# A decoder of six stages on one core: earlier first product, three changed orders, and cross-attention with its PSUM banks dealt out anew

## The chip, the core and the metric

The kernel runs on one core of a Trainium2 chip, in one launch. The time is that of the device, in microseconds: the median of 3 runs, 1364.35 us (1364.26 to 1366.4). The core has TensorE (PE, matrix products and transposes, results in PSUM only), VectorE (DVE), ScalarE (ACT), GpSimd (POOL) and SyncE (SP, which issues transfers here). Each runs its own list of instructions in order, and they wait for each other on semaphores. PSUM has eight banks, each with 512 float32 a partition; the kernel keeps two engines out of one bank at a time by waits.

## The reference

x holds 16 blocks of 128 tokens with 256 channels, ctx the same of context. Six residual layers follow each other:

```
x = x + channel_attention(layernorm(x))          # softmax over channels, 256x256 scores per block
x = x + cross_attention(layernorm(x), ctx)       # 32 heads of 8, RMS-normalised q and k
x = x + quantised_linear(layernorm(x))           # rounded activations and weight
x = x + linear_attention(layernorm(x))           # 16 heads, decay, gate, group norm
x = x + gated_convolution(ctx, ctx, layernorm(x))
x = x + grouped_attention_and_experts(layernorm(x))  # 16 heads on 4 key heads; 8 experts, 2 per token
```

Cross-attention, with the block's 128 tokens and 128 context rows:

```
q = x @ Wq.T ; kv = ctx @ [Wk; Wv].T  (k and v interleaved)
q, k = rmsnorm(q), rmsnorm(k)         # over the 8 channels of a head
out = softmax(q k^T / sqrt(8)) v
```

## The kernel before

Each stage is a function with one list a stage for each engine, and ends with a barrier of all engines. The stages are: the first loads, channel attention (names `ca.`), cross-attention with the quantised linear layer (`xa.`, `ql.`), linear attention (`la.`), the convolution (`cv.`), grouped attention with the router (`ga.`), and the experts (`ex.`). TensorE's first work in them is at 15.53, 145.79, 334.64, 512.88, 611.71 and 1113.34 us.

A stage is a software pipeline over the 16 blocks. `steps` calls `step(s)` for each s, from some lead steps on to some steps behind the last, and in it `s.back(1)` is the block one earlier, `s.back(-1)` the one after. So a step works on several blocks, and the order of the parts within `step` is the order on the engine. `upto(b)` is the semaphore's value once block b is done. There is no planner: what stands first in the code is first on its engine, and whatever stands behind a wait waits too.

**Loads** (lines 215 to 236). SyncE issues x in three parts (blocks 0, 1 to 3, 4 to 15). ScalarE issues the identity and four weights. All four weights count into one semaphore, and TensorE waits for 64 of it before its first instruction (line 392). The next stages' weights follow on SyncE at once (from line 287).

**Channel attention.** In a step TensorE does the transpose of xn (line 400), psc for the block before (408), pout for the one before that (418), then pqk and pv (426, 432), and pmix (442), which waits for wo. wo is made by VectorE (342) from the row sums of ScalarE's exponentials (374), and these need the negated maxima (324, 326) of psc. VectorE does the addition of pout to x (320) ahead of the maxima.

**Cross-attention.** The bank `turn` serves in a step for the transposed xn, for pv's product with the probabilities (po) and for the v product; `turn2` for the transposed q and k, later for the turned output; `pqk` for q and k side by side. q and k are copied to raw and squared (668, 671), VectorE sums the squares (604), GpSimd takes ten operations for the root (106 to 124), and VectorE scales to `qkn` (586). TensorE turns it (724), VectorE spreads qT (597), and ScalarE copies kT (663). These two read one bank, so ScalarE waits for VectorE.

**Grouped attention.** For a block there are five products k/q (`kq`, 1717), each rotated: VectorE by cos (1551), ScalarE swaps the halves (`swap`, 1635 and 1636), GpSimd adds up (1498, 1506). The four rounds r of the block before go scores, exponentials, transposes, values (paT, 1742), `copy_aT` (1658). The output product (1761) needs all four aT.

## Time and profile before

| | us |
|---|---|
| median of 3 runs (lowest, highest) | 1364.35 (1364.26, 1366.4) |
| profiled execution | 1367.16 |
| its span, first to last instruction | 1364.7 |
| TensorE busy (matrix products) | 1186.6 (87%) |
| TensorE busy (weight loads) | 832.2 (61%) |
| VectorE busy | 765.1 (56%) |
| ScalarE busy | 577.8 (42%) |
| GpSimd busy | 603.6 (44%) |

The mean granted clock of TensorE is 0.955 of 2.4 GHz. Each stage has other limits, so the shares over the whole say little. In 700 to 1080 us, within grouped attention, TensorE is busy for 361.37 of 380 us; in 180 to 400 us, most of it cross-attention and linear attention, for 182.15 of 220. A wait costs time only where the engine that waits is the one that sets the pace. Times of matrix products in the timeline include the last one's way through the array, so the next may begin before the end shown.

### The profile page before, as it was taken

Reading aid. Unit: us, or ns where it says so; the run is one execution under the profiler, and the core shown is the slowest. Engines: PE = TensorE matmul, PEld = TensorE weight load, DVE = VectorE, ACT = ScalarE, POOL = GpSimd, SP = SyncE. Lnnn points to the kernel's source line nnn. Section 1 sums busy time; section 2 is a strip of 40 time slices with the busy share of each in tenths; the row PEclk is TensorE's granted clock in tenths of the full one; section 3 lists DMA queues with packets and bytes.
Section 4 is the critical chain, followed back from the end, with each engine's and each line's share of the span. In section 5 each row is a group of like instructions: output and inputs, shape, how many; then the busy total and the mean of one; then the engine's idle time right before and its main releaser. Section 6 shows DMA issues by size and latency. Waiting matters only on the chain. (4 is left out here: it accounts for less than half of the span.)

```text
span 1364.7 us, 24627 instructions
## 1 busy us (share of the span) xinstructions
PE 1186.6 (87%) x7421; PEld 832.2 (61%) x7422; DVE 765.1 (56%) x1930; ACT 577.8 (42%) x1504; POOL 603.6 (44%) x752
## 2 busy tenths in 40 slices
PE   4888588885899969978999999999999859999995
PEld 3666355563555534436878888878888626665663
DVE  2444368875788857984566666666666532222221
ACT  1333266663333320004666566666566413333331
POOL 1000245552555536745666556666565312233222
PEclk9999699997999989988999999999999869999998
DMA  6000000000699204014000000000000312322223
GB/s 249 1 0 0 12 12 13 15 12 2 152 206 206 58 1 160 0 40 210 1 9 17 16 13 12 15 12 15 15 13 13 147 35 39 46 46 43 43 44 85
DMA packets 46353, 69.40 MB, mean 51 GB/s; under 512 B 4736, under 2 KB 42672, under 8 KB 45232
## 3 DMA queue, kind: packets, MB, share of 16 engines
q1 hardware_dynamic: 36864, 52.69, 14.5%
q0 software_dynamic: 7152, 9.34, 4.2%
q10 hardware_dynamic: 2272, 6.56, 1.3%
q8 instruction: 34, 0.56, 0.2%
q14 instruction: 31, 0.25, 0.1%
HBM read 57.12 MB, written 32.58 MB: 66 GB/s over the span
## 5 line engine op out<-in xcount | busy, mean ns | idle before, releaser
L1717 PE MATMUL ga.pkq<-ga.xnT,g.early 128*128 128x128 f32 x1280 | 156.7, 276 | 1.0 <-ACT ga.halves L1636 1.0
L1717 PEld LDWEIGHTS ga.pkq<-ga.xnT,g.early 128*128 128x128 f32 x1280 | 151.4, 193 | 9.6 <-issue 8.2
L1761 PE MATMUL ga.turn_out<-g.early,ga.aT 128*128 128x256 f32 x512 | 119.1, 386 | 10.8 <-ACT ga.aT L1658 10.8
L1498 POOL TENSOR_TENSOR ga.halves<-ga.halves,g.ga_sinT 128x512 f32<-128x512 f32 x80 | 104.3, 1304 | 50.9 <-ACT ga.halves L1636 50.9
L1761 PEld LDWEIGHTS ga.turn_out<-g.early,ga.aT 128*128 128x128 f32 x512 | 95.5, 191 | 25.6 <-issue 8.8
L1506 POOL TENSOR_TENSOR ga.kqT<-ga.by_cos,ga.halves 128x512 f32<-128x512 f32 x80 | 101.7, 1272 | 16.5 <-issue 16.5
L1551 DVE TENSOR_TENSOR ga.by_cos<-ga.pkq,g.ga_cosT 128x512 f32<-128x512 f32 x80 | 55.3, 691 | 95.6 <-PE ga.pkq L1717 51.5
L1643 ACT ACTIVATE ga.e<-ga.psc,ga.negmax 128x128 f32<-128x128 f32 x256 | 90.4, 366 | 40.6 <-DVE ga.negmax L1564 39.7
L1872 DVE TENSOR_TENSOR ex.hidden<-ex.silu,ex.p 128x512 f32<-128x512 f32 x39 | 26.8, 688 | 124.8 <-PE ex.p L1925 118.4
L1742 PE MATMUL ga.paT<-ga.pT,ga.v 128*128 128x512 f32 x128 | 68.7, 619 | 13.9 <-ACT ga.pT L1651 10.0
L1920 PE MATMUL ex.p<-g.spare,ex.xnT 128*128 x156 | 76.9, 616 | 1.1 <-ACT ex.xnT L1900 0.8
L1849 POOL TENSOR_TENSOR ex.token<-ex.token_d,ex.zero 128x1 uint32<-128x1 uint32 x39 | 7.0, 178 | 155.4 <-DVE ex.y L1878 144.9
L1942 PE MATMUL ex.py<-g.late,ex.hT 128*128 x312 | 73.9, 380 | 0.8 <-ACT ex.hT L1906 0.8
L1925 PE MATMUL ex.p<-g.early,ex.xnT 128*128 x156 | 74.2, 599 | 0.0
L1108 POOL TENSOR_TENSOR g.spare<-g.ctxT 128x1024 f32<-128x1024 f32 x32 | 60.5, 1892 | 28.0 <-PE cv.y L1188 28.0
L1635 ACT ACTIVATE ga.halves<-ga.pkq 64x512 f32<-64x512 f32 x80 | 47.5, 593 | 58.6 <-DVE ga.by_cos L1551 57.5
L1853 POOL DMA_INDIRECT mo_acc<-ex.y,ex.token x39 | 60.8, 1558 | 18.2 <-issue 18.2
L1726 PE MATMUL ga.psc<-ga.kqT 128*128 128x128 f32 x512 | 66.2, 278 | 2.9 <-POOL ga.kqT L1506 2.9
L655 ACT ACTIVATE g.late<-xa.ps 128x2048 f32<-128x2048 f32 x32 | 60.1, 1878 | 19.5 <-PE xa.ps L716 19.5
L1726 PEld LDWEIGHTS ga.psc<-ga.kqT 128*128 128x128 f32 x512 | 61.9, 194 | 3.5 <-POOL ga.kqT L1506 3.1
L1942 PEld LDWEIGHTS ex.py<-g.late,ex.hT 128*128 128x128 f32 x312 | 56.3, 190 | 7.5 <-issue 1.5
L1270 POOL TENSOR_TENSOR ga.root<-ga.ss,g.minus_half 128x1 f32<-128x1 f32 x16 | 9.0, 564 | 110.6 <-DVE ga.ss L1296 110.6
(288 smaller groups left out, 2634.2 us busy)
## 6 DMA issues: line engine op xcount, KB each, us to landing
mo_rows<-in_pad_rows SPq DMA_DIRECT2D x1, 18447.0 KB, 99.6
ex.row<-mo_rows SPq DMA_DIRECT2D x39, 129.0 KB, 2.1
g.spare<-in_mo_w SPq DMA_DIRECT2D x1, 4096.0 KB, 12.3
g.late<-in_mo_w SPq DMA_DIRECT2D x1, 4096.0 KB, 22.7
g.early<-in_mo_w SPq DMA_DIRECT2D x1, 4096.0 KB, 12.6
g.ctxT<-in_ctxR SPq DMA_DIRECT2D x1, 2048.0 KB, 12.7
xa.ctxT<-in_ctxT SPq DMA_DIRECT2D x16, 128.0 KB, 2.5
g.spare<-cv_rows SPq DMA_DIRECT2D x1, 2048.0 KB, 7.7
```

Source lines behind the costliest of these rows:

```text
L1108: return nc.gpsimd.tensor_tensor(g.cv_kv[:, u % 2, :].rearrange("p (m j i) -> p m j i", j=8, i=8), spread(v, 3, 8), spread(v, 2, 8), ALU.mult)
L1498: nc.gpsimd.tensor_tensor(by_sin[:, par, :].rearrange("p (h t) -> p h t", h=REP), halves[:, par, :].rearrange("p (h t) -> p h t", h=REP), ...
L1506: nc.gpsimd.tensor_tensor(kqT[:, s.par, r, :], by_cos[:, par, :], by_sin[:, par, :], ALU.add).then_inc(kqT_ready, 1)
L1643: last = nc.scalar.activation(e[:, r % 2, j * P:(j + 1) * P], psc[:, r % 2, j * P:(j + 1) * P], ACT.Exp, bias=negmax[:, r % 2, j:j + 1], s ...
L1717: last = nc.tensor.matmul(pkq[:, par, j * P:(j + 1) * P], w[:, q, at * P:(at + 1) * P], xnT[:, s.par, q, :], start=(q == 0), stop=(q == C ...
L1726: last = nc.tensor.matmul(psc[:, r % 2, j * P:(j + 1) * P], kqT[:, b.par, r + 1, j * P:(j + 1) * P], kqT[:, b.par, 0, r * P:(r + 1) * P], ...
L1742: nc.tensor.matmul(paT[:], v[:, b.par, r * P:(r + 1) * P], pT[:, r % 2, :], start=True, stop=True).then_inc(pv_done, 1)
L1761: last = nc.tensor.matmul(pout, aT[:, h // REP, (h % REP) * P:(h % REP + 1) * P], g.ga_wo[:, h, :], start=(h == 0), stop=(h == H - 1))
L1853: nc.gpsimd.indirect_dma_start(g.acc, bass.IndirectOffsetOnAxis(ap=token[:, b.par, :], axis=0), y[:, b.par, :], None, compute_op=ALU.add). ...
L1920: last = nc.tensor.matmul(p1[:], xnT[:, t.par, c, :], g.mo_w1[:, bass.ds(expert, 1), c, :].rearrange("p e f -> p (e f)"), start=(c == 0), ...
L1925: last = nc.tensor.matmul(p3[:], xnT[:, t.par, c, :], g.mo_w3[:, bass.ds(expert, 1), c, :].rearrange("p e f -> p (e f)"), start=(c == 0), ...
L1942: last = nc.tensor.matmul(py[:, 0:D], hT[:, f * P:(f + 1) * P], g.mo_w2[:, bass.ds(expert, 1), f, :].rearrange("p e d -> p (e d)"), start= ...
```

## The change

**Loads.** k's weight moves to SyncE's queue, between the first two parts of x. The third part of x and all of the next stages' weights wait until the last weight of channel attention has landed. TensorE waits for q's and k's weights ahead of the first pqk, for v's ahead of the first pv; VectorE for wo ahead of its first use. The identity's bf16 copy moves into channel attention.

**Three orders.** Channel attention: VectorE takes the maxima ahead of the addition to x. Grouped attention: ScalarE's copy of aT(3) comes ahead of the last swap, and TensorE turns the next block's xn in round 2 instead of round 3.

**Cross-attention.** The v product goes to the q half of the bank `pqk`, for the newest block, once q and k are copied out. The k product comes first in a step. The turned k lies in the bank `turn`, so ScalarE's copy of kT no longer waits for VectorE's qT. The next transpose of xn no longer waits for v's copy. In its place, the pv products wait for kT, and q, k and v products for each other's copies.

**Semaphores.** GpSimd clears those of cross-attention in step 2 of linear attention.

TensorE, the last step of cross-attention ahead of the loop. `xa.qkn` is the scaled q and k, `xa.ctxT` marks the k product where it goes to `xa.pqk` ahead of the q product, and the v product behind the turn of `xa.oT`. Before:

```order
L724 MATMUL xa.turn<-g.ident,xa.qkn 128x128 x4
L731 MATMUL xa.pqk<-g.early,xa.ctxT 128x256 x2
L734 MATMUL xa.pqk<-g.early,xa.xnT 128x256 x2
L741 MATMUL xa.pc<-g.ident_bf,ql.xq 128x128 x2
L752 MATMUL xa.turn<-g.late,g.spare 32x128 x32
L716 MATMUL xa.ps<-xa.qT,xa.kT 128x512 x4
L767 MATMUL xa.pc<-ql.wq,ql.xqT 128x256 x2
L772 MATMUL xa.turn<-g.ident,xa.oT 128x128 x4
L776 MATMUL xa.turn<-g.early,xa.ctxT 128x256 x2
L783 MATMUL xa.turn<-g.ident,xa.xn 128x128 x2
L716 MATMUL xa.ps<-xa.qT,xa.kT 128x512 x4
```

And now:

```order
L739 MATMUL xa.pqk<-g.early,xa.ctxT 128x256 x2
L747 MATMUL xa.turn<-g.ident,xa.qkn 128x128 x2
L749 MATMUL xa.turn<-g.ident,xa.qkn 128x128 x2
L754 MATMUL xa.pqk<-g.early,xa.xnT 128x256 x2
L761 MATMUL xa.pc<-g.ident_bf,ql.xq 128x128 x2
L774 MATMUL xa.turn<-g.late,g.spare 32x128 x32
L731 MATMUL xa.ps<-xa.qT,xa.kT 128x512 x4
L789 MATMUL xa.pc<-ql.wq,ql.xqT 128x256 x2
L794 MATMUL xa.turn<-g.ident,xa.oT 128x128 x4
L799 MATMUL xa.pqk<-g.early,xa.ctxT 128x256 x2
L804 MATMUL xa.turn<-g.ident,xa.xn 128x128 x2
L731 MATMUL xa.ps<-xa.qT,xa.kT 128x512 x4
```

The k product stood behind the transposes of `xa.qkn` and now stands ahead of them; the transposes go to two banks (both in the name `xa.turn`); the v product keeps its place and goes to the bank `xa.pqk`.

VectorE in channel attention, one step from the maxima on. Before:

```order
L320 TENSOR_TENSOR g.x<-ca.pout,g.x 128x256
L324 TENSOR_REDUCE ca.negmax<-ca.psc 128x2
L326 TENSOR_SCALAR ca.negmax<-ca.negmax 128x2
L251 TENSOR_SCALAR ca.xn<-g.x,ca.mv,ca.rstd 128x256
L337 RECIPROCAL ca.rowsum<-ca.rowsum 128x2
L342 TENSOR_SCALAR ca.wo<-g.early,ca.rowsum 128x256 x2
L242 BN_STATS ca.stats<-g.x 128x6
```

And now:

```order
L327 TENSOR_REDUCE ca.negmax<-ca.psc 128x2
L329 TENSOR_SCALAR ca.negmax<-ca.negmax 128x2
L334 TENSOR_TENSOR g.x<-ca.pout,g.x 128x256
L254 TENSOR_SCALAR ca.xn<-g.x,ca.mv,ca.rstd 128x256
L344 RECIPROCAL ca.rowsum<-ca.rowsum 128x2
L351 TENSOR_SCALAR ca.wo<-g.early,ca.rowsum 128x256 x2
L245 BN_STATS ca.stats<-g.x 128x6
```

The addition to x has gone behind the maxima.

ScalarE at the end of a step of grouped attention, from the copy of xnT to the exponentials. Before:

```order
L1697 ACTIVATE ga.xnT<-ga.turn_out,g.ga_norm 128x128 x2
L1635 ACTIVATE ga.halves<-ga.pkq 64x512
L1636 ACTIVATE ga.halves<-ga.pkq 64x512
L1635 ACTIVATE ga.halves<-ga.pkq 64x512
L1636 ACTIVATE ga.halves<-ga.pkq 64x512
L1658 ACTIVATE ga.aT<-ga.paT 128x512
L1399 ACTIVATE ga.hnT<-ga.router,g.mo_norm 128x128 x2
L1643 ACTIVATE ga.e,ga.inv<-ga.psc,ga.negmax 128x128 x8
```

And now:

```order
L1721 ACTIVATE ga.xnT<-ga.turn_out,g.ga_norm 128x128 x2
L1659 ACTIVATE ga.halves<-ga.pkq 64x512
L1660 ACTIVATE ga.halves<-ga.pkq 64x512
L1682 ACTIVATE ga.aT<-ga.paT 128x512
L1659 ACTIVATE ga.halves<-ga.pkq 64x512
L1660 ACTIVATE ga.halves<-ga.pkq 64x512
L1423 ACTIVATE ga.hnT<-ga.router,g.mo_norm 128x128 x2
L1667 ACTIVATE ga.e,ga.inv<-ga.psc,ga.negmax 128x128 x8
```

The last aT stands ahead of the last pair of halves.

```diff
@@ load_first
         def _(sp):
-            for k in range(len(X_PARTS) - 1):
-                part = slice(X_PARTS[k], X_PARTS[k + 1])
-                sp.dma_start(g.x[:, part, :], h["x"][:, part, :]).then_inc(g.x_loaded[k], 16)
+            load_x(g, sp, 0)
+            sp.dma_start(g.ca_wqk[:, :, D:2 * D], h["ca_wk"]).then_inc(g.ca_qk_loaded, 16)
+            load_x(g, sp, 1)
...
         def _(pool):
             nc.gpsimd.memset(g.minus_half[:], -0.5).then_inc(g.fill, 1)
-            pool.wait_ge(g.ident_loaded, 16)
-            nc.gpsimd.tensor_copy(g.ident_bf[:], g.ident[:]).then_inc(g.fill, 1)
@@ channel_attention
         def _(sp):
+            sp.wait_ge(g.ca_o_loaded, 16)
+            load_x(g, sp, 2)
...
         def _(dve):
-                b = s.back(2)
-                if b.on:
-                    dve.wait_ge(out_done, upto(b))
-                    nc.vector.tensor_tensor(g.x[:, b.i, :], pout[:, 0:D], g.x[:, b.i, :], ALU.add).then_inc(x_added, 1)
                 b = s.back(1)
...
+                b = s.back(2)
+                if b.on:
+                    dve.wait_ge(out_done, upto(b))
+                    nc.vector.tensor_tensor(g.x[:, b.i, :], pout[:, 0:D], g.x[:, b.i, :], ALU.add).then_inc(x_added, 1)
...
+                    if b.base is None and b.n == 0:
+                        dve.wait_ge(g.ca_o_loaded, 16)
...
         def _(pe):
             pe.wait_ge(g.ident_loaded, 16)
-            pe.wait_ge(g.ca_loaded, 16 * g.ca_loads)
...
+                    if s.base is None and s.n == 0:
+                        pe.wait_ge(g.ca_qk_loaded, 32)
...
+                    if s.base is None and s.n == 0:
+                        pe.wait_ge(g.ca_v_loaded, 16)
@@ cross_attention_and_quantised_linear
-        pv, po = turn[:, D:2 * D], turn[:].rearrange("p (g n) -> p g n", g=4)
+        po = turn[:].rearrange("p (g n) -> p g n", g=4)
+        pv = pqk[:, 0:D]
...
         def _(act):
                     act.wait_ge(qk_turned, upto(b))
-                    act.wait_ge(qT_ready, upto(b))
-                    nc.scalar.activation(kT[:, b.par, :, :], turn2[:, 1, :, :], ACT.Copy).then_inc(kT_ready, 1)
+                    nc.scalar.activation(kT[:, b.par, :, :], turn[:, 0:D], ACT.Copy).then_inc(kT_ready, 1)
...
-                if b.on:
-                    act.wait_ge(v_done, upto(b))
+                if s.on:
+                    act.wait_ge(v_done, upto(s))
+                    if s.past(2):
+                        act.wait_ge(pv_done, upto(s, back=2))
...
         def _(pe):
+                if s.on:
+                    pe.wait_ge(ctx_loaded[s.par], upto_half(s))
+                    if s.past(1):
+                        pe.wait_ge(raw_ready, upto(s, back=1))
+                        pe.wait_ge(v_ready, upto(s, back=1))
+                    for k in range(C):
+                        nc.tensor.matmul(pqk[:, D:2 * D], ctxT[:, s.par, k, :], g.xa_wk[:, k, :], start=(k == 0), stop=(k == C - 1))
                 if b.on:
                     pe.wait_ge(qk_ready, upto(b))
...
+                    if s.on:
+                        pe.wait_ge(xnT_ready, upto(s))
+                    for k in range(C):
+                        nc.tensor.transpose(turn2[:, 0, k, :], qkn[:, k * P:(k + 1) * P], g.ident[:])
+                    for k in range(C):
+                        last = nc.tensor.transpose(turn[:, k * P:(k + 1) * P], qkn[:, D + k * P:D + (k + 1) * P], g.ident[:])
...
                     pe.wait_ge(exp_done, upto(a, per=2))
+                    if b.on:
+                        pe.wait_ge(kT_ready, upto(b))
...
-                if b.on:
+                if s.on:
+                    pe.wait_ge(raw_ready, upto(s))
                     for k in range(C):
-                        last = nc.tensor.matmul(pv, ctxT[:, b.par, k, :], g.xa_wv[:, k, :], start=(k == 0), stop=(k == C - 1))
+                        last = nc.tensor.matmul(pv, ctxT[:, s.par, k, :], g.xa_wv[:, k, :], start=(k == 0), stop=(k == C - 1))
...
-                    if b.on:
-                        pe.wait_ge(v_ready, upto(b))
@@ linear_attention, GpSimd
+                if s.base is None and s.n == 2:
+                    for sem in g.finished_next:
+                        nc.gpsimd.sem_clear(sem)
@@ grouped_attention
                     swap(s, 3)
+                if b.on:
+                    copy_aT(b, 3)
+                if s.on:
                     swap(s, 4)
-                if b.on:
-                    copy_aT(b, 3)
...
-                    if r == KV - 1 and n.on:
+                    if r == 2 and n.on:
                         pe.wait_ge(xn_ready, upto(n))
```

## Rows read from the trace of the kernel before

**Rows 1.** The page's first line.

```profile
span 1364.7 us, 24627 instructions
```

**Rows 2.** Timeline, start of the program: start us, us, engine, line, work, [idle before, releaser].

```profile
3.11 0.68 ACTq L230 DMA_DIRECT2D g.early<-in_ca_wo  x1
...
4.25 0.43 DVE L242 BATCH_NORM_STATS2 ca.stats<-g.x 128x6 f32<-128x256 f32 x1 [4.25 <-PEq L217]
...
15.53 0.66 PE L400 MATMUL ca.turn<-g.ident,ca.xn 128*128 128x128 f32 x2 [15.53 <-DMA g.early<-in_ca_wo]
...
16.67 3.78 PE L426 MATMUL ca.pqk<-g.early,ca.xnT 128*128 128x512 f32 x4 [0.47 <-ACT ca.xnT L367]
```

**Rows 3.** DMA view, 0 to 40 us, a column a us; issues with us to landing.

```profile
GB/s 0 23 276 243 276 360 408 376 393 253 356 403 399 414 410 393 378 404 394 435 406 426 442 377 246 16 0 0 0 0 0 0 0 0 0 0 0 0 0 0
...
g.early<-in_ca_wq ACTq DMA_DIRECT2D x1, 256.0 KB, 9.4
```

**Rows 4.** Timeline, one step of channel attention.

```profile
57.58 1.03 PE L408 MATMUL ca.psc<-ca.qk 128*128 128x256 f32 x4
...
59.63 0.42 DVE L320 TENSOR_TENSOR g.x<-ca.pout,g.x 128x256 f32 x1 [2.96 <-PE ca.pout L418]
...
59.97 0.68 DVE L324 TENSOR_REDUCE ca.negmax<-ca.psc 128x2 f32<-128x512 f32 x1
...
61.02 1.05 PE L432 MATMUL ca.pv<-ca.xnT,g.early 128*128 128x128 f32 x8
...
62.32 0.62 DVE L342 TENSOR_SCALAR ca.wo<-g.early,ca.rowsum 128x256 f32<-128x256 f32 x2
...
62.99 1.99 PE L442 MATMUL ca.pmix<-ca.wo,ca.w 128*128 128x256 f32 x8 [0.91 <-DVE ca.wo L342]
```

**Rows 5.** Waits, whole program: engine, line, waited for; us, times, longest.

```profile
PE ca.pmix L442 <- DVE ca.wo L342: 15.6, 16, 3.3
```

**Rows 6.** Timeline, last pmix of channel attention.

```profile
136.50 3.12 PE L442 MATMUL ca.pmix<-ca.wo,ca.w 128*128 128x256 f32 x8 [3.31 <-DVE ca.wo L342]
```

**Rows 7.** Timeline, one step of cross-attention.

```profile
232.96 1.03 PE L734 MATMUL xa.pqk<-g.early,xa.xnT 128*128 128x256 f32 x4
...
233.80 0.38 ACT L663 ACTIVATE xa.kT<-xa.turn 128x256 f32<-128x256 f32 x1 [0.92 <-DVE xa.qT L597]
...
234.70 0.69 DVE L604 TENSOR_REDUCE xa.msq<-xa.sq 128x64 f32<-128x512 f32 x1 [0.25 <-ACT xa.sq L668]
...
240.28 1.08 DVE L586 TENSOR_TENSOR xa.qkn<-g.spare,xa.norm 128x512 f32<-128x512 f32 x1
...
250.25 0.99 DVE L586 TENSOR_TENSOR xa.qkn<-g.spare,xa.norm 128x512 f32<-128x512 f32 x1 [0.52 <-POOL xa.norm L124]
```

**Rows 8.** Waits, 180 to 310 us.

```profile
DVE xa.msq L604 <- ACT xa.sq L668: 3.4, 13, 0.3
```

**Rows 9.** Timeline, cross-attention's first steps.

```profile
170.81 1.91 PE L731 MATMUL xa.pqk<-g.early,xa.ctxT 128*128 128x256 f32 x4
...
174.47 0.60 ACT L668 ACTIVATE xa.sq<-xa.pqk 128x512 f32<-128x512 f32 x1 [1.71 <-PE xa.pqk L734]
```

**Rows 10.** Timeline, end of a step of grouped attention.

```profile
713.85 0.59 ACT L1635 ACTIVATE ga.halves<-ga.pkq 64x512 f32<-64x512 f32 x1 [1.32 <-DVE ga.by_cos L1551]
...
715.07 0.60 ACT L1658 ACTIVATE ga.aT<-ga.paT 128x512 f32<-128x512 f32 x1
...
715.81 3.69 PE L1761 MATMUL ga.turn_out<-g.early,ga.aT 128*128 128x256 f32 x16 [0.82 <-ACT ga.aT L1658]
...
725.15 0.60 ACT L1676 ACTIVATE ga.v<-ga.ppT 128x512 f32<-128x512 f32 x1 [0.17 <-PE ga.ppT L1770]
```

**Rows 11.** Waits, 650 to 1090 us.

```profile
PE ga.turn_out L1761 <- ACT ga.aT L1658: 10.8, 16, 1.0
```

**Rows 12.** Timeline, POOL at the start of cross-attention and in linear attention.

```profile
144.33 0.20 POOL L528 MEMSET ql.ones<- 128x128 f32 x1 [28.06 <-issue]
...
353.49 3.04 POOL L866 TENSOR_TENSOR la.norm<-la.msq,g.minus_half 128x16 f32<-128x16 f32 x1 [1.59 <-DVE la.msq L914]
```

More of the change, by code:

```diff
@@ L212, in fill_value_windows, with load_x @@
         nc.gpsimd.memset(vd[:, k, :, 0:512].rearrange("p q (g z) -> p q g z", z=32)[:, :, :, 8:16], 1.0)
+def load_x(g, eng, k):
+    part = slice(X_PARTS[k], X_PARTS[k + 1])
+    eng.dma_start(g.x[:, part, :], g.h["x"][:, part, :]).then_inc(g.x_loaded[k], 16)
 def load_first(nc, g, h):
@@ L226, in _ @@
             act.dma_start(g.ident[:], h["ident"]).then_inc(g.ident_loaded, 16)
[L227 to L230 removed]
+            act.dma_start(g.ca_wqk[:, :, 0:D], h["ca_wq"]).then_inc(g.ca_qk_loaded, 16)
+            act.dma_start(g.ca_wv, h["ca_wv"]).then_inc(g.ca_v_loaded, 16)
+            act.dma_start(g.ca_wo, h["ca_wo"]).then_inc(g.ca_o_loaded, 16)
         @block.gpsimd
@@ L301, in step @@
                 if s.base is None and s.n == 2:
+                    pool.wait_ge(g.ident_loaded, 16)
+                    nc.gpsimd.tensor_copy(g.ident_bf[:], g.ident[:]).then_inc(g.fill, 1)
                     fill_value_windows(nc, pool, g.xa_vd)
@@ L511, in cross_attention_and_quantised_linear @@
             "xqT_ready", "y_done", "y_added", "w_sum_ready", "wq_ready", "filled"))
+        g.finished_next = m.sems + n.sems
         block = ctx.enter_context(nc.Block())
@@ L721, in step @@
                         pe.wait_ge(o_ready, upto(b, back=2))
-                    for t in range(2):
-                        for k in range(C):
-                            last = nc.tensor.transpose(turn2[:, t, k, :], qkn[:, t * D + k * P:t * D + (k + 1) * P], g.ident[:])
+                    if s.on:
[4 more added lines that the diff above has]
+                        last = nc.tensor.transpose(turn[:, k * P:(k + 1) * P], qkn[:, D + k * P:D + (k + 1) * P], g.ident[:])
                     last.then_inc(qk_turned, 1)
                 if s.on:
-                    pe.wait_ge(ctx_loaded[s.par], upto_half(s))
-                    if s.past(1):
-                        pe.wait_ge(raw_ready, upto(s, back=1))
-                    for k in range(C):
-                        nc.tensor.matmul(pqk[:, D:2 * D], ctxT[:, s.par, k, :], g.xa_wk[:, k, :], start=(k == 0), stop=(k == C - 1))
                     pe.wait_ge(xnT_ready, upto(s))
@@ L1700, in step @@
                     swap(s, 3)
-                    swap(s, 4)
                 if b.on:
                     copy_aT(b, 3)
+                if s.on:
+                    swap(s, 4)
             steps(act, step, 1, 4)
```

12 lines of the change are left out of this document (4 added, 8 removed).

## The prediction

> **What bounds the kernel now.** I read the page first, for the span and the stages [rows 1], then the timeline stage by stage at each stage that the diff touches, and last the table of waits, to learn how often a wait seen in one step comes back. The profiled execution took 1367.16 us, 1364.7 of it span and 2.5 around it. That is 2.8 above the median of the runs, 1364.35. The stages follow each other behind barriers, so what each one saves adds up. In channel attention and grouped attention TensorE is nearly full, and its few waits are path. In cross-attention the path goes round from VectorE to GpSimd and back, with TensorE waiting. Before 15.5 us nothing but transfers runs.
>
> **1. The start.** TensorE's first transpose is at 15.53, released by the last of four weight loads, and the first product at 16.67 [rows 2]. VectorE began at 4.25 and had long finished; a 256 KB weight of ScalarE's queue took 9.4 us to land, because 1.5 MB of x and the next stages' weights move beside it [rows 3]. Now the 1.5 MB wait for the last weight, each product waits for its own weight alone, and ScalarE issues one transfer fewer (0.6 of the 0.68 that the last one takes, [rows 2]) before the barrier. VectorE's start moves from 4.25 to 3.6. Its chain to the end of the first normalised batch (statistics, GpSimd's root, the scaling) took 2.0 us by the timeline, to 6.29, while TensorE was still held; so the transpose can run at 5.65, and the product, 1.14 later as before, at 6.8. Are q's and k's weights there by then? x's first batch, the identity and both weights are 704 KB; three batches of x may share the line, making 1.1 MB. The columns of [rows 3] add up to 0.82 MB at 5 us and 1.18 MB at 6 us. Yes, at 5 to 6 us. v's weight and wo, 1.64 MB in all, are there at some 7 us and needed at 10 or later. The rest of x, issued at about 8, lands by 15; VectorE asks for it in the third step, near 22. Saved: 16.67 - 6.8 = 9.9. The bounds: the weights can't come as late as now, since the 1.5 MB now start behind them; if the product had to wait for all 1.64 MB and 2 us of latency, 9.2 us, the gain is 7.5. I take 9.9, and 7.5 to 10.4 as its range.
> These bytes are worked out from the columns alone. The Trainium skill ("DMA: Bandwidth & Descriptors", section "Queues, rings and completion order") says that each DMA engine takes turns between queues, packet by packet. The trace agrees: the queue with long x packets moved 2 MB before 320 KB of the other had landed. By that rule q and k, now in both queues with equal packets, land at 5 us; the sum would be the same.
>
> **2. Channel attention: the maximum ahead of the addition.** psc is finished at 58.61 (57.58 + 1.03), but the reduction starts at 59.97, since the addition to x stands ahead of it and waits for pout [rows 4]. From the reduction's start to pmix are 3.02 us (59.97 to 62.99). Put first, the reduction starts at 58.7 and pmix could at 61.7. TensorE is busy with v until 62.07 (61.02 + 1.05), so its 0.91 wait goes entirely, with some 0.3 to spare. The addition now starts at 59.65 as before, in the hole while ScalarE takes the exponentials. All 16 such waits are 15.6 us [rows 5]. The first, 0.37, has no addition and stays. The last, 3.31 [rows 6], shrinks by 1.27 to 2.04, because TensorE has nothing else there. 15.6 - 0.4 - 2.0 = 13.2. Bounds: 10 if one of ScalarE's copies comes late instead, 15.4 if the last pmix and pout (3.12 and 2.07, against 1.99 and 1.03 when the clock is full) come before the clock falls. I take 13.2.
>
> **3. Cross-attention.** In a steady step the scaled q and k (qkn) start at 240.28 and again at 250.25 [rows 7]: 9.97. In between VectorE works through its list, waits for ScalarE's square (0.25 before the reduction at 234.70), hands a seed to GpSimd, and GpSimd's ten small operations end right at the next qkn. The square waits for two things that the change takes away: kT's copy, held 0.92 by VectorE's qT because both lie in one bank, and the q product, which stands behind the k product. With kT in its own bank and the k product done while TensorE waits for qkn, the square comes some 0.8 earlier and VectorE no longer waits. But no more than its own wait can go: the loop is then VectorE and GpSimd alone. So the k product (1 us a step) buys only 3.4 us in 13 steps [rows 8]. TensorE's wait before the transpose of xn, which v in the bank of q and k removes, turns into a longer wait for qkn.
> The first three steps differ, because GpSimd and TensorE alternate with the clock at half. There the k product takes 1.70 (170.81 to the q product at 172.51) and VectorE waits for the square at 174.47 [rows 9]. Step 1 saves 1.6 for the k product; the weight's quantisation needs scores(1), which come 2.1 earlier, as v's copy no longer stands ahead of the transpose; step 2 saves 1.7 more: 3.8. In the tail there is no q product to cover the wait of the pv products for kT: -0.3. Sum 3.8 + 3.4 - 0.3 = 6.9, with 2 and 14 as bounds.
> The Trainium skill ("SBUF — State Buffer", section "Who interferes with whom") says that a VectorE operation with two SBUF inputs and a GpSimd operation that reads SBUF exclude each other. By that rule a shift of VectorE against GpSimd can lengthen either; in the trace qkn takes 1.08 and 0.99. If it ate the steady gain, cross-attention would give 3.5.
>
> **4. Linear attention.** 36 semaphores are cleared on GpSimd ahead of norm in step 2. The 17 cleared before the memset at 144.33 took at most 1.2 us from the stage's start at 143.1: 70 ns each, 2.5 us here. GpSimd had 1.59 idle there [rows 12]; the 0.9 left delays norm, whose reader on VectorE then still has the mask product before it until 357.7. Price 0, at most 1.
>
> **5. Grouped attention.** At a step's end ScalarE does swap(4) at 713.85 after 1.32 idle, then aT(3) at 715.07 to 715.67, and the output product waits 0.82 for it at 715.81 [rows 10]. paT(3) is ready at 713.0, so aT(3) fits into the idle time, to 713.65, and swap(4) still starts at 713.85. The product starts right behind the scores. 16 waits, 10.8 us [rows 11]; the last, 0.26, has no swap. What is late next: v's copy, at 725.15 [rows 10] after 0.17 of waiting for its product, ends at 725.6 then, and TensorE asks for it at 726.63 - 0.82 = 725.8. It fits by 0.2. The transpose of xn one round earlier moves 0.22 of TensorE's work and removes no wait: 0. Taken: 10.5, range 6 to 11.
>
> **Sum.** 9.9 + 13.2 + 6.9 + 0 + 10.5 = 40.5. The profiled execution would take 1326.7, the median 1364.35 - 40.5, rounded 1324. With each part at its own edge the ends lie at 24 and 52 saved (1340, 1312); not all go one way, so 1317 to 1331 for this case.
>
> **Rivals.**
> (a) TensorE bounds cross-attention, and the whole k product comes off: 13 steps by 1.0 us instead of 3.4, so 9.6 more, 1314. For it: TensorE waits less than VectorE works. Against: in [rows 7] nothing of TensorE's stands between the seed and qkn.
> (b) Grouped attention gives nothing: v's copy or the negated maxima, which ScalarE must do between, come late as TensorE arrives 0.8 sooner, and the wait moves there. 1324 + 10.5 = 1334.5. For it: only 0.2 of slack. Against: v's own copy waits for TensorE too.
> (c) Cross-attention gives nothing: GpSimd's chain stretches by what VectorE gains, and the half clock stays on longer as TensorE's work is spread. 1331.
> (d) Slower: aT(3) now holds swap(4). If paT(3) came later than cos(4) by more than the idle 1.32, the rotation on GpSimd, then the next scores, would be late in each of 16 steps. It decides against the whole from 40.5 / 16 = 2.5 us a step, that is 3.8 us behind today's. At 4 us it gives 1364 + 24 = 1388. Against: paT(3) leads cos(4) by 0.1 to 0.8.
> (e) The change doesn't do what it says: the start still hangs on one late load and the orders wait elsewhere; within 0.2%.
>
> **Numbers.** Forecast 0.60, (a) 0.10, (b) 0.14, (c) 0.10, (d) 0.04, (e) 0.02. The range 1315 to 1336 leaves out (d), (e), and most of (a). About 0.2%, 2.7 us, is what a measurement of this kernel can tell from no change. Faster 0.94, same 0.02, slower 0.04.
>
> **What would show it.** The first product at 6.8 (wrong if after 9); no wait before pmix but in the first and last step, a period of 6.5 instead of 7.4; in cross-attention no wait of VectorE for the square, a step of 9.65, and TensorE waiting over 1 us for qkn; in linear attention norm late by 0.9 and nothing behind it; in grouped attention no wait for aT before the output product, a step of 28.1 instead of 28.9. The forecast is wrong if TensorE's wait reappears under another name in either attention, or if a step of cross-attention is under 9.3.

## The result and the profile after

The changed kernel takes 1322.88 us, median of 5 runs (1320.28 to 1323.33), against 1366.4 (1364.26 to 1369.21) for the kernel before, run beside it. The ratio is 0.967, 95% interval 0.9651 to 0.9689. The forecast was 1324, with 40.5 saved from 1364.35; 43.5 were, from 1366.4. The profiled execution took 1320.28.

First the page of the changed kernel, its span and busy times:

```profile
span 1318.3 us, 24667 instructions
PE 1182.8 (90%) x7421; PEld 831.5 (63%) x7422; DVE 774.4 (59%) x1930; ACT 580.5 (44%) x1504; POOL 603.9 (46%) x752
```

TensorE has the same work as before in 46.4 us less span: what went is waiting. The stages follow each other, so the first TensorE work of each splits the span. The table holds these differences for five of the profiles, each read from its timeline; the experts' row ends at the start of TensorE's last products. The last three columns are the changed kernel with one part undone. "Stretch" below is the time between two such marks, and a stage's "drain" is its end, where no new block comes and TensorE has little to fill its waits with: in cross-attention from the last transposes of q and k on, in grouped attention from the last product of v on.

| us | before | changed | addition first | aT(3) last | cross-attention old |
|---|---|---|---|---|---|
| start, to the first transpose | 15.53 | 5.55 | 5.56 | 5.55 | 5.55 |
| channel attention | 130.26 | 111.72 | 130.18 | 112.93 | 113.02 |
| cross-attention | 188.85 | 184.67 | 185.61 | 182.71 | 192.01 |
| linear attention | 178.24 | 178.88 | 178.64 | 178.13 | 178.41 |
| convolution | 98.83 | 98.96 | 98.70 | 98.84 | 98.78 |
| grouped attention | 501.63 | 487.88 | 485.19 | 498.12 | 487.69 |
| experts | 234.68 | 234.09 | 233.80 | 234.71 | 234.76 |

The same code in two columns can differ by 2 to 3 us; the section on the experiments comes back to that.

Timeline of the changed kernel, the start, against [rows 2]:

```profile
3.36 0.43 DVE L245 BATCH_NORM_STATS2 ca.stats<-g.x 128x6 f32<-128x256 f32 x1 [3.36 <-PEq L223]
...
5.55 0.66 PE L408 MATMUL ca.turn<-g.ident,ca.xn 128*128 128x128 f32 x2 [5.55 <-DVE ca.xn L254]
...
6.68 3.60 PE L436 MATMUL ca.pqk<-g.early,ca.xnT 128*128 128x512 f32 x4 [0.47 <-ACT ca.xnT L376]
```

The transpose waits for VectorE, no longer for a transfer, and the product starts at 6.68 (forecast 6.8). VectorE itself starts at 3.36, before at 4.25, since fewer transfers are issued ahead of the first barrier.

Timeline of the changed kernel, one step of channel attention, against [rows 4]; behind it the weight load's row of the kernel before at the same place:

```profile
62.26 1.03 PE L416 MATMUL ca.psc<-ca.qk 128*128 128x256 f32 x4
...
63.33 0.69 DVE L327 TENSOR_REDUCE ca.negmax<-ca.psc 128x2 f32<-128x512 f32 x1 [2.13 <-PE ca.psc L416]
...
64.31 0.42 DVE L334 TENSOR_TENSOR g.x<-ca.pout,g.x 128x256 f32 x1
...
65.71 1.05 PE L444 MATMUL ca.pv<-ca.xnT,g.early 128*128 128x128 f32 x8
...
66.60 1.89 PE L454 MATMUL ca.pmix<-ca.wo,ca.w 128*128 128x256 f32 x8
```

```profile
62.99 1.59 PEld L442 LDWEIGHTS ca.pmix<-ca.wo,ca.w 128*128 128x128 f32 x8 [1.10 <-DVE ca.wo L342]
```

The reduction starts right behind psc, and pmix 0.89 after pv's start with no wait. Before, that distance was 1.97. The difference, 1.08, is near the 1.10 of the weight load's row and not the 0.91 of the product's row: the latter counts from the end of the last product of pv, which the profile models and puts 0.19 later. Steady steps took 7.36 and 7.45 in turn before and take 6.28 now, 1.12 less (6.5 was announced).

Waits of VectorE for the square, before and changed, over cross-attention (us, times, longest):

```profile
DVE xa.msq L604 <- ACT xa.sq L668: 12.6, 16, 3.9
```

```profile
DVE xa.msq L618 <- ACT xa.sq L681: 6.2, 3, 3.9
DVE xa.qkn L600 <- POOL xa.norm L124: 11.1, 11, 4.6
```

The waits of the 13 steady steps are gone [rows 8]. TensorE now waits 0.95 and 0.68 in turn ahead of the transposes of q and k, less than the "over 1 us" that was announced. A steady step takes 9.58 instead of 9.89.

Timeline of the changed kernel, grouped attention at the place of [rows 10]:

```profile
707.16 0.60 ACT L1682 ACTIVATE ga.aT<-ga.paT 128x512 f32<-128x512 f32 x1 [0.26 <-PE ga.paT L1767]
707.86 0.59 ACT L1659 ACTIVATE ga.halves<-ga.pkq 64x512 f32<-64x512 f32 x1
```

```profile
707.17 1.95 PE L1751 MATMUL ga.psc<-ga.kqT 128*128 128x128 f32 x16
708.96 3.62 PE L1786 MATMUL ga.turn_out<-g.early,ga.aT 128*128 128x256 f32 x16
```

aT(3) is copied in ScalarE's old idle time, the swap stands 0.10 behind it, and the output product starts 1.79 after the scores, before 2.78 (715.81 - 713.03). Steps of 28.92 and later 29.03 to 29.09 became 27.86 and 28.02 (28.1 was announced).

### The profile page after: what moved, and what is told of

Its sections match the earlier page's. It is cut to its first block and busy times, and to the rows that moved or that the text cites. A ratio compares the mean times of both kernels' runs of the same rounds, so it can differ in the third digit from the quotient of the medians.

```text
span 1318.3 us, 24667 instructions
## 1 busy us (share of the span) xinstructions
PE 1182.8 (90%) x7421; PEld 831.5 (63%) x7422; DVE 774.4 (59%) x1930; ACT 580.5 (44%) x1504; POOL 603.9 (46%) x752
## 5 line engine op out<-in xcount | busy, mean ns | idle before, releaser
L1132 POOL TENSOR_TENSOR g.spare<-g.ctxT 128x1024 f32<-128x1024 f32 x32 | 60.6, 1893 | 28.1 <-PE cv.y L1212 28.1
L1950 PEld LDWEIGHTS ex.p<-g.early,ex.xnT 128*128 128x128 f32 x156 | 30.2, 194 | 38.4 <-issue 38.4
## 6 DMA issues: line engine op xcount, KB each, us to landing
g.spare<-in_mo_w SPq DMA_DIRECT2D x1, 4096.0 KB, 12.1
g.ctxT<-in_ctxR SPq DMA_DIRECT2D x1, 2048.0 KB, 11.9
```

Source lines behind the costliest of these rows:

```text
L1132: return nc.gpsimd.tensor_tensor(g.cv_kv[:, u % 2, :].rearrange("p (m j i) -> p m j i", j=8, i=8), spread(v, 3, 8), spread(v, 2, 8), ALU.mult)
L1950: last = nc.tensor.matmul(p3[:], xnT[:, t.par, c, :], g.mo_w3[:, bass.ds(expert, 1), c, :].rearrange("p e f -> p (e f)"), start=(c == 0), ...
```

## The experiments

All are the changed kernel with one edit. Times are medians of 4 runs; ratios go to the kernel before, which ran beside them (1367.2 to 1367.8). Three variants whose edits turned out worth nothing (below) and the changed kernel lie at 1319.2 to 1322.9, mean 1320.95; "above the changed one" means above that mean. By this mean and the 1367.2 to 1367.8 of the kernel before, the change saves some 46.5, more than the 43.5 of the first comparison.

### Channel attention: the addition first again

```
+                b = s.back(2)   # out_done, g.x += pout: ahead of the maxima
                 b = s.back(1)   # scores_done, maxima
-                b = s.back(2)
```

> The changed kernel with VectorE's addition to x ahead of the maxima again in channel attention. Channel attention took 111.7 us in the changed kernel (first transpose 5.55 to cross-attention's 117.27), 130.3 before; the forecast gave the order 13.2. Theory: a wait costs 0.2 more than the row of the matrix products shows, since that row counts it from the modelled end of the last product; the weight load's row before pmix shows the full 1.1. All 18.5 belong to the order then: a step takes 7.41 instead of 6.28, the row of the products shows 0.9 before pmix, the last pmix takes 3.1 at half clock, the stage 130.3, the kernel 1322.9 + 18.5 = 1341.4. Rival: the order is worth the forecast's 13.2 and the rest came from the start (weights and x that land at other times): 125.0 for the stage, 1336, and steps of 7.2.

Measured: 1335.65, ratio 0.9768 (0.9737 to 0.9799), 14.7 above the changed one. Stage 130.18, steady steps of 7.36 and 7.45, as in the kernel before to 0.1. The rival's stage of 125.0 and step of 7.2 are out: by the stage the whole difference is the order's, and nothing came from the start. The total alone would have said otherwise, since it is the rival's 1336 and not the theory's 1341.4. Of the stage's 18.5, 14.6 lie between the first and the last psc (109.39 against 94.81). The last pmix:

```profile
126.89 2.67 PE L454 MATMUL ca.pmix<-ca.wo,ca.w 128*128 128x256 f32 x8 [3.31 <-DVE ca.wo L351]
```

At 2.67 it ran partly at half clock (granted 0.72 of 2.4 GHz over it). The forecast's upper bound was that with the new order, and its shorter wait of 2.02, the clock would hold. It does not always. The same product in the changed kernel, in that with aT(3) last and in that with cross-attention as before, whose code is the same up to here:

```profile
110.03 1.99 PE L454 MATMUL ca.pmix<-ca.wo,ca.w 128*128 128x256 f32 x8 [2.02 <-DVE ca.wo L351]
```

```profile
109.97 3.28 PE L454 MATMUL ca.pmix<-ca.wo,ca.w 128*128 128x256 f32 x8 [2.02 <-DVE ca.wo L351]
```

```profile
109.66 3.67 PE L454 MATMUL ca.pmix<-ca.wo,ca.w 128*128 128x256 f32 x8 [2.02 <-DVE ca.wo L351]
```

The same eight products behind the same wait take 1.99, 3.28 and 3.67, with a granted clock of 1.00, 0.58 and 0.54. Whether the clock has fallen there differs from execution to execution.

The medians show 14.7 for the order where the stage shows 18.5, or 17.3 against the mean of the changed order in eleven profiles without extra products in this stage (111.35 to 114.38, mean 112.9). The 2.6 between 17.3 and 14.7 are in grouped attention, whose drain ran at full clock in this profile (stage 485.19 instead of 487.8). Whether it does so in its other runs no profile shows.

### Grouped attention: the two edits apart

```
                 if s.on:
-                if b.on:
-                    copy_aT(b, 3)
                     swap(s, 4)
+                if b.on:
+                    copy_aT(b, 3)
```

> The changed kernel with ScalarE's copy aT(3) behind swap(4) again; the transposes of xn stay in round 2. Theory: the copy's place is all of the stage's gain, 13.7, because the 0.82 that the row of the products shows before the output product costs 1.0: step 28.9 instead of 27.9, kernel 1336.6. Rival: the copy is worth the forecast's 10.5 and the transposes' place the other 3.2: step 28.7, kernel 1333.4. In both the row of the output product shows 0.8 again.

Measured: 1331.78, ratio 0.9752 (0.9724 to 0.978), 10.8 above; the theory's 1336.6 and the rival's 1333.4 are both higher. From the first to the last product of v 427.14 instead of 415.0: 12.1 for 15 steps, 0.8 each. The stage shows 10.2, since the first half of the last output product ran at full clock in this profile (3.72 instead of 5.05), and the drain was shorter with it. TensorE's waits in 620 to 1020 us:

```profile
PE ga.turn_out L1786 <- ACT ga.aT L1682: 8.9, 14, 0.7
```

Again a wait costs more in the step than in the row: 0.64 on average here, while the step takes 28.78 instead of 27.86.

```
-                    if r == 2 and n.on:
+                    if r == KV - 1 and n.on:
```

> The changed kernel with TensorE's transposes of the next block's xn in round 3 of grouped attention again; aT(3) stays ahead of swap(4). With both, 15 steps took 415.0 us (first to last product of v); with aT(3) behind swap(4) and the transposes in round 2 427.1; before, 429.6. Theory: the transposes' place is worth the small rest, 0.1 a step: 416.7, steps of 28.1, kernel 1.7 above the changed one. Rival (the forecast): it is worth nothing, 415.0, and the 2.5 between 429.6 and 427.1 were the clock.

Measured: 1320.82, ratio 0.9661 (0.9645 to 0.9677), the time of the changed kernel. The stretch is 414.83. The rival, which was the forecast, is right: with aT(3) early the transposes' place is worth nothing. Beside this kernel the one before differs by aT(3) alone in this stage, and takes 429.62: the copy's place alone is worth 14.8, 0.99 a step, where the row shows 0.82. While aT(3) is late, the transposes in round 2 seem worth 2.5 (429.62 against 427.14); TensorE waits 8.9 for aT in 620 to 1020 us, 10.8 before, which is 1.9 of it, and one odd step of 29.75 in the kernel before is the rest.

### Cross-attention: which part does what

```
-def cross_attention_and_quantised_linear(nc, g):   # as changed
+def cross_attention_and_quantised_linear(nc, g):   # as before
```

> The changed kernel with cross-attention as before; start and the other orders stay. Theory: the changed stage saves 3.4 in the first three steps and 4.0 in the steady ones and loses 3.2 in the tail, where TensorE's clock is at half for the last two blocks' value products (3.41 and 3.11 instead of 1.95). Without it the stage takes 188.9 instead of 184.7, its tail stays at full clock, the kernel takes 1327.1. Rival: the tail falls to half clock whatever the order, and the forecast's 6.9 was right: stage 191.6, kernel 1329.8.

Measured: 1328.85, ratio 0.9722 (0.9697 to 0.9747), 7.9 above. From the stage's first transpose to the last transposes of q and k 164.83, before 164.76, changed 157.40. The 7.4 are near the forecast's 3.8 + 3.4. The rest of the stage, its drain, took 27.18 here, 24.09 in the kernel before with the same code: so the "loses 3.2 in the tail" of the theory is not the new order's alone, and its 4.2 for the stage was too small. The rival was right that the tail can fall to half clock in either order, and near with its total. The value products of the last two blocks, before, changed, and here:

```profile
311.44 1.95 PE L752 MATMUL xa.turn<-g.late,g.spare 128*32 128x128 f32 x64
...
319.75 1.95 PE L752 MATMUL xa.turn<-g.late,g.spare 128*32 128x128 f32 x64 [1.68 <-ACT g.late L655]
```

```profile
275.89 3.41 PE L774 MATMUL xa.turn<-g.late,g.spare 128*32 128x128 f32 x64 [0.45 <-ACT xa.kT L676]
...
285.83 3.11 PE L774 MATMUL xa.turn<-g.late,g.spare 128*32 128x128 f32 x64 [1.87 <-ACT g.late L669]
```

```profile
284.29 3.40 PE L765 MATMUL xa.turn<-g.late,g.spare 128*32 128x128 f32 x64
...
294.05 3.62 PE L765 MATMUL xa.turn<-g.late,g.spare 128*32 128x128 f32 x64 [1.87 <-ACT g.late L668]
```

Then the three parts. Turned k beside q again:

```
-  nc.tensor.transpose(turn[:, k * P:(k + 1) * P], qkn[:, D + ...
+  nc.tensor.transpose(turn2[:, 1, k, :], qkn[:, D + ...
+  act.wait_ge(qT_ready, upto(b))      # ahead of kT's copy, which reads turn2
-  pe.wait_ge(kT_ready, upto(b))       # ahead of the value products
```

> The changed kernel; in cross-attention only the turned k goes back beside the turned q, so that kT's copy waits for VectorE's qT. The k product first and v's new place stay. Theory: the k product first gives the gain of the first steps (10.8 and 10.4 instead of 12.5 and 12.1), and in the steady steps kT's copy makes the square 0.2 to 0.3 late: 9.75 a step instead of 9.61, the stretch 159.5, the kernel 1325. Rival: the bank of kT alone is what frees VectorE: steady steps 9.87, the stretch 161, 1326.5; other rival: the k product does it alone, steady steps 9.61, 157.5, 1323.

Measured: 1325.21, ratio 0.9693 (0.9677 to 0.9709), 4.3 above. The steady step is 9.88 and the stretch 161.43, as the first rival had them. One more run, meant to put the k product back as well, did not: what ran was this same kernel, so its expectation tells of another one. It is given as a second measurement of this kernel.

> The changed kernel; in cross-attention only the v product keeps its new place (bank of q and k, newest block). The k product stands behind the transposes again, and the turned k lies beside the turned q, so kT's copy waits for VectorE's qT. From the stage's first transpose to the last transpose of q and k the old order took 164.8, the changed one 157.4 (156.7 and 158.2 in two other runs). Theory: v's place gives nothing by itself; the steady pair of steps takes 19.75 again (9.87 each), the second and third step 12.4 and 12.1, the stretch 164.5, the kernel 1330. Rival: v's copy out of the way makes the weight's quantisation earlier and gives some 2 in the first steps: 162.5, 1328.

Measured for that: 1325.22 (1320.36 to 1327.8), ratio 0.9682 (0.9656 to 0.9707).

Next the k product goes back behind the transposes, first with the turned k in its own bank, then with the turned k beside q as well, so that v's place alone is left:

```
-  k product (ctx_loaded, raw_ready, v_ready; pqk[:, D:2 * D]) ahead of the transposes of qkn
+  the same lines behind them, ahead of the q product
```

> The changed kernel; in cross-attention only the k product goes back behind the transposes of q and k. The turned k keeps its bank, v its place. The steady step was 9.88 with the k product first and the turned k beside q, 9.57 with both. Theory: both are needed, since the square waits for the later of kT's copy and the q product: 9.8 a steady step, the stretch 161 to 162, the kernel 1325. Rival: the bank of kT does it alone, 9.57 steady, 158, 1322.

> The changed kernel; in cross-attention only the v product keeps its new place. The k product stands behind the transposes of q and k, the turned k lies beside the turned q. With the k product first as well, two profiles showed 24.6 become 21.3 and 20.7 from the first to the third transposes, and 9.88 a steady step as in the old order (9.89). Theory: the gain of the first steps is v's place (its copy no longer holds the transposes of xn, and the weight's quantisation behind them) and little of the k product: 22 for the three, 9.88 steady, the stretch to the last transposes 162, the kernel 1326. Rival (the forecast): the k product at half clock is the gain: 24.6 for the three, 164.8, 1329.

Measured: 1327.5, ratio 0.9705 (0.968 to 0.973), and 1329.33, ratio 0.9725 (0.9698 to 0.9752). The two medians are within each other's spread; what tells the kernels apart is the timelines. In one table (us):

| k product | turned k | first to third transposes of q, k | steady step | to the last of them |
|---|---|---|---|---|
| behind | beside q, v old | 24.62 | 9.89 | 164.76 |
| behind | beside q | 24.16 | 9.94 | 165.04 |
| behind | own bank | 24.12 | 9.92 | 164.72 |
| first | beside q | 21.33, 20.69 | 9.88, 9.88 | 161.43, 160.81 |
| first | own bank | 21.22 | 9.58 | 157.40 |

Six more profiles hold the changed cross-attention up to its drain: they show 18.98 to 22.19 for the first steps, 9.56 to 9.58 a steady step, and 155.17 to 158.23 to the last transposes. So the first steps differ by up to 3 us between executions of the same code, and the steady step hardly at all.

The k product first gives some 3 us in the first steps, with either place of the turned k. A bank for the turned k gives 0.3 a steady step, but only with the k product first. v's place alone gives nothing; whether the other two need it was not run. VectorE's wait for the square says the same. With the k product first and the turned k beside q:

```profile
DVE xa.msq L618 <- ACT xa.sq L682: 8.8, 16, 3.9
```

With the k product behind and the turned k in its own bank:

```profile
DVE xa.msq L618 <- ACT xa.sq L681: 12.6, 16, 3.9
```

The 3.8 between 12.6 and 8.8 belong to the first steps, with 16 waits left; the last 2.6 go only when both are changed. The forecast had both parts right. What it said of v's copy, that its new place brings scores(1) 2.1 earlier, gives little by itself: v's place alone turned 24.62 into 24.16. My theories in between, that v's place gives the first steps' gain, and that with the k product behind its own bank keeps some of the steady one, were wrong.

### The start: do the 1.5 MB matter?

The hold of SyncE for the last weight is taken out; in a second run the third part of x is issued at once, ahead of the barrier.

```
-            sp.wait_ge(g.ca_o_loaded, 16)
             load_x(g, sp, 2)
```

> The changed kernel; SyncE no longer waits for the last weight of channel attention before it issues the third part of x and the next stages' weights. Theory (the forecast's): the 1.5 MB made the weights late. q's and k's lead their queues and are nearly there, the first product moves from 6.7 to 7 to 9, v's weight and wo land after 10, and the kernel is 2 to 4 slower, 1326. Rival: what moved the first product was that it no longer waits for all four weights, and the hold is idle: 6.7, 1323, within 1 us.

> The changed kernel; the third part of x (1.5 MB) is issued at once behind the second, ahead of the first barrier, as before the change; the rest of the new start stays. Theory (the forecast's): these bytes made the weights late. q's weight lands at some 9 to 10 instead of 6, the first product starts at 9.5, the kernel is 3 slower, 1325. Rival: with every product waiting for its own weight it makes no difference: 6.7, 1322.

Measured: 1319.19, ratio 0.9642 (0.9626 to 0.9658); 1320.92, ratio 0.9666 (0.9644 to 0.9687). Both are the changed kernel's time. The first product starts at 6.68 without the hold. With x at once, the timeline has

```profile
7.14 3.75 PE L435 MATMUL ca.pqk<-g.early,ca.xnT 128*128 128x512 f32 x4 [0.69 <-DMA g.early<-in_ca_wq]
```

That is 0.46 late: the transpose before it starts 0.24 later, as VectorE starts behind one more issue, and q's weight takes the other 0.22. Transfers of the kernel before, and of the one with x at once (KB, us from issue to landing):

```profile
g.early<-in_ca_wq ACTq DMA_DIRECT2D x1, 256.0 KB, 9.4
g.early<-in_ca_wk ACTq DMA_DIRECT2D x1, 256.0 KB, 10.1
g.early<-in_ca_wv ACTq DMA_DIRECT2D x1, 256.0 KB, 10.8
g.early<-in_ca_wo ACTq DMA_DIRECT2D x1, 256.0 KB, 12.3
```

```profile
g.early<-in_ca_wk SPq DMA_DIRECT2D x1, 256.0 KB, 4.4
g.early<-in_ca_wq ACTq DMA_DIRECT2D x1, 256.0 KB, 5.9
...
g.early<-in_ca_wv ACTq DMA_DIRECT2D x1, 256.0 KB, 4.8
g.early<-in_ca_wo ACTq DMA_DIRECT2D x1, 256.0 KB, 9.8
```

With the 1.5 MB in flight, wo, issued at 2.45, lands at 12.25; with the hold it takes 5.8 and lands at 8.25; before, issued at 3.11, it landed at 15.4. q's weight takes 1.1 longer than with the hold (4.8), but k's, now ahead of x's second and third part in SyncE's queue, is there after 4.4. So what frees the start is that a product waits for its own weight, and that k's weight stands ahead of most of x; the hold is worth at most 0.46, which the totals don't show. How the gain divides between the two was not run. In the rows of the kernel before, q's weight had landed at 10.55 and k's, issued at 1.80, at 11.9; by my estimate from these, separate waits alone would have given the first product at about 12, and the other 5 us would be due to the new place of k's weight.

### Spare products: the clock in the drains

"Spare" products are ones whose results nobody reads; they only keep TensorE at work. In the drain of cross-attention TensorE repeats a k product in this way, in waits of 1.68, 1.31 and 1.87.

```
+                if b.on and not s.on:
+                    spare_products(1)     # ahead of the transposes, and of scores(1)
+                if a.on and not b.on:
+                    spare_products(2)     # ahead of the value products
```

> The changed kernel, and in the tail of cross-attention, where no new block comes, TensorE repeats the last k product into the bank of q and k, which nobody reads any more: one pair ahead of the last transposes of q and k, one ahead of the last scores, two ahead of the last value products. They lie in TensorE's waits of 1.68, 1.31 and 1.87. Theory: the tail's loss is the clock. It stays at full, the value products take 1.95 twice, the stage is 2.6 to 3.1 shorter (181.8), the kernel 1320. Rival: the loss is the new wait for kT and the longer chain; then nothing is won, 1323, or up to 0.9 lost where a spare pair is in the way.

Measured: 1318.83, ratio 0.965 (0.9625 to 0.9674), runs of 1318.5 to 1319.5. The value products:

```profile
277.86 1.95 PE L784 MATMUL xa.turn<-g.late,g.spare 128*32 128x128 f32 x64 [0.45 <-ACT xa.kT L676]
286.18 1.98 PE L784 MATMUL xa.turn<-g.late,g.spare 128*32 128x128 f32 x64
```

The drain took 24.42; in ten profiles with v's new place and without spare products 25.7 to 27.5, in the old order 24.09 once and 27.18 once. Both value products ran with a granted clock of 1.00, where the changed kernel had 0.55 and 0.60. So the drain's loss is the clock, and 0.3 is left of it, which fits the forecast's price for the wait for kT. Whether the new order makes the fall likelier, two profiles of the old one can't tell. The total lies 2.1 below the mean, at the edge of what can be told.

Then the same at the seams of nearly all stages:

```
+def spare_turns(nc, g, to, times):
+    for _ in range(times):
+        nc.tensor.transpose(to[:, 0:P], g.ident[:], g.ident[:])
```

> The changed kernel with spare work for TensorE where it waits at the seams: turns of the identity into a bank that nobody reads ahead of the first transpose of each stage but the convolution (8 to 18 of them), 18 each in the waits of the drains of linear and grouped attention, k products repeated in the first two steps and the drain of cross-attention. The results that are read stay the same. Theory: the stages' starts and drains run at half clock, by a chance that differs between executions, and cost 8 to 12 in all; the spare work gives most of it back: 1312, and the runs lie closer together. Rival: what is spare is in the way, or the clock falls whatever TensorE does: 1322 or slower.

Measured: 1305.3 (1300.86 to 1310.62), ratio 0.955 (0.9513 to 0.9587), 15.7 below the mean, with all of TensorE's spare work in it; 8 to 12 were expected. It beats both kernels. The runs don't lie closer together, against the expectation. First products of linear attention, changed and with spare work:

```profile
303.08 3.78 PE L1061 MATMUL la.pqk<-g.early,la.xnT 128*128 128x512 f32 x4 [0.47 <-ACT la.xnT L989]
```

```profile
297.55 1.28 PE L218 MATMUL la.turn<-g.ident 128*128 128x128 f32 x10 [1.60 <-DVE g.early L932]
299.36 0.44 PE L1067 MATMUL la.turn<-g.ident,la.xn 128*128 128x128 f32 x2 [0.52 <-DVE la.xn L260]
300.27 1.98 PE L1084 MATMUL la.pqk<-g.early,la.xnT 128*128 128x512 f32 x4 [0.47 <-ACT la.xnT L1011]
```

The granted clock over the first product is 0.50 in the changed kernel and 1.00 here. Counted from each stage's first transpose behind the spare ones, linear attention took 173.56 instead of 178.88, the convolution 97.15 instead of 98.96, grouped attention 482.6 instead of 487.9, cross-attention 181.1 instead of 184.7. In this kernel cross-attention's drain took 25.13, with both value products at full clock and more spare products in the way. At the very start and before the experts the first products gained nothing: they took 3.78 and 3.77, against 3.60 and 3.78 without.

## Why the prediction was right

The time was hit, and the large edits did what was forecast, by the waits that were named. Two terms were too small, and that the total came so near is in part luck. Term by term:

- **Start, 9.9.** 9.98 by the timeline. The cause was half right: separate waits and the place in the queue, yes; the 1.5 MB that "now start behind them", no, at most 0.46. So the lower bound, which leaned on those bytes, had a wrong reason. The rule of the Trainium skill ("DMA: Bandwidth & Descriptors", "Queues, rings and completion order"), that engines take turns between queues packet by packet, gave q and k at 5 us; they landed 4.8 and 4.4 after an issue at 1.15, at 5.95 and 5.55. Before, x's 2 MB did not land ahead of the 320 KB, as the forecast read it: the last part of x was issued at 1.62 and took 9.2, so it landed at 10.8, and q's weight at 10.55.
- **Channel attention, 13.2.** 17.3 to 18.5 in the stage: mis-sized, and past the upper bound of 15.4. The step that failed is the pricing of a wait by the product's row. Fourteen waits are 0.2 longer each, 2.7 in all: 14.6 are saved from the first to the last psc, where their rows add up to 11.9. (The Trainium skill, "TensorE: Matmul & The Clock Gate", "Single matmul latency", puts a single bf16 product's way through the array at roughly 0.175 us; the products here are float32, and the rows agree with their 0.19.) Of the rest of the 18.5, 1.3 is what the last wait lost, as forecast, and 2.1 is the clock in the last pmix and pout, which the forecast had in its upper bound and which differs between executions. The last 0.6 lies ahead of the first psc, a piece that took 5.30 to 7.34 in the profiles.
- **Cross-attention, 6.9.** 7.4 up to the drain, by the two parts named (3.4 and 4.0 for 3.8 and 3.4). The stage in the changed kernel's profile shows 4.2 only, as the value products in its drain ran near half clock (drain 27.27 against 24.09) and those of the kernel before did not. The medians show 7.9. The step that was announced as 9.65 is 9.58, and the limit of 9.3 was not passed. Against rival (c), qkn takes 1.08 and 0.99 as before, and GpSimd's chain for the root takes 4.3 in both kernels. So the exclusion of VectorE and GpSimd ("SBUF — State Buffer", "Who interferes with whom", of the Trainium skill) took nothing that shows from the steady gain.
- **Linear attention, 0.** Right, and cheaper than thought: GpSimd waited 1.64 before norm, where it had waited 1.59 [rows 12], so the 36 clears fit in it, at most 46 ns each. The 70 ns from [rows 12] were a bound, used as a price; "norm late by 0.9" did not come.

```profile
321.26 2.99 POOL L890 TENSOR_TENSOR la.norm<-la.msq,g.minus_half 128x16 f32<-128x16 f32 x1 [1.64 <-DVE la.msq L938]
```

- **Grouped attention, 10.5.** 14.8 for aT(3) by the stretch of 15 steps, 13.75 for the stage: mis-sized, and past the range of 6 to 11. The same step failed: a step gained 0.99 where the row shows 0.82, 2.6 in 15 steps. Another 0.9 is a wait for aT that stands in the row of the values' product (`ga.paT`, line 1742). The rest is some 1 us of other waits of TensorE that fell. 0 for the transposes of xn was right. v's copy, the announced next one to be late, fitted: TensorE's waits for it are 0.8 in 4 steps.

The two mis-sized terms came to some 8 too little. In the profiles cross-attention's drain took 3.2 of that back, and the span shrank by 46.4, 6 more than the sum. The time came nearer than this for two reasons that the forecast had no part in: it started from 1364.35, where the same kernel took 1366.4 and later 1367.2 to 1367.8, and the 1322.88 lies 2 above the mean of the kernels that are worth the same. Medians of one kernel differ by that much.

Two smaller slips of the forecast changed nothing. With each part at its own edge the saving is 24.5 to 50.8 by its own bounds, not 24 to 52. And before 15.5 us not only transfers run: VectorE works from 4.25 on, as the forecast's own first term says.

## What to carry to other kernels

Price a wait of TensorE by the distance between the starts of the products on either side of it, or, as in channel attention, by the weight load's row, not by the idle time in the product's row: here 0.2 of each wait was missing there, 5 us over 29 waits. Where an engine waits for the later of two things that end at one time, as the square for kT's copy and the q product, making either one early gives nothing (9.92 and 9.88 a step) and only both together give the gain (9.58); try the pairs before one is called useless. And compare stages by their steady stretch, apart from start and drain, since these change by 1 to 3 us between executions with the clock.

## What the runs showed of the hardware

- The same products behind the same or nearly the same waits ran at full clock (2.4 GHz) in one execution and partly or wholly at half (1.2 GHz) in another: the last pmix 1.99, 3.28, 3.67; the last but one value products of cross-attention 1.95 or 3.41, with a granted clock of 1.00 or 0.55; the first half of grouped attention's last output product 3.72 or 5.05, with 1.00 or 0.73. TensorE had waited 1.7 to 2.7 us at least once shortly before each. The last of these, in the kernel with the addition first and in the changed one:

```profile
1058.86 3.72 PE L1786 MATMUL ga.turn_out<-g.early,ga.aT 128*128 128x256 f32 x16 [0.47 <-ACT ga.aT L1682]
```

```profile
1041.48 5.05 PE L1786 MATMUL ga.turn_out<-g.early,ga.aT 128*128 128x256 f32 x16 [0.26 <-ACT ga.aT L1682]
```

  The Trainium skill ("TensorE: Matmul & The Clock Gate", "What's actually happening") says of the clock's rise that it varies between runs of one kernel; these rows show it of the fall, too.
- Work that nobody reads, put into TensorE's waits at the seams, took the program from 1320.95 to 1305.3, and its mean granted clock in the profiles from 0.956 to 0.978 of 2.4 GHz. Turning an identity 8 times in 1.94 us before the first stage did not raise the clock for what followed; 18 times in 4.08 us before grouped attention did (v product 1.98 instead of 3.78).
